# The second value head of a pair kept with its two batches exchanged

## The reference, cut to what matters

```
attn  = inverse of (I + strictly lower part of (k_beta k^T * decay))        64 x 64
w     = attn (v_beta - k_beta*g_exp state)                                  "solve"
out   = (q*g_exp) state + lower(q k^T * decay) w                            "inter" + "intra"
state = state*g_last + (k * k_decay)^T w                                    128 x 128
y     = rmsnorm(out * silu(z)) ; result += y W_out[its 128 rows]
```

## Time and profile before

| what | value |
|---|---|
| runs, us | 4985.07, 4973.11, 4982.58; median 4982.58 |
| the profiled execution, us | 4975.11; its span in the trace 4973.3 |
| mean granted TensorE clock | 0.985 of full speed |
| busy: TensorE matmuls, weight loads, DVE, ACT, GpSimd | 93%, 64%, 72%, 62%, 22% |
| instructions: matmul records, weight loads | 54288, 54320 |

### The profile page before, as it was taken

How to read it: one execution, slowest core, us unless ns; L and a number is a source line. 1 busy time by engine, 2 the same in 40 slices (tenths; PEclk the granted TensorE clock), 3 DMA queues, 4 the chain that set the end, 5 groups by cost and what they waited for, 6 DMA issues and landing times.

```text
span 4973.3 us, 144942 instructions
## 1 busy us (share of the span) xinstructions
PE 4647.1 (93%) x54288; PEld 3181.4 (64%) x54320; DVE 3576.1 (72%) x6424; ACT 3061.3 (62%) x7979; POOL 1089.0 (22%) x1064
## 2 busy tenths in 40 slices
PE   4998899999999899999999899999999899999998
PEld 2555666666666566666666566666666666666666
DVE  7554677777777577777777677777777677777775
ACT  2333666666666566666666566666666566666665
POOL 0000122222222122222222122222222222222222
PEclk8999999999999999999999999999999999999999
DMA  2111222222223222222223222222223322222221
GB/s 61 37 38 62 65 68 55 60 66 61 66 58 75 65 68 51 62 67 61 66 52 80 69 55 60 66 61 67 55 60 82 69 58 59 64 66 61 68 55 37
DMA packets 760109, 305.29 MB, mean 61 GB/s; under 512 B 672880, under 2 KB 716016, under 8 KB 749168
## 3 DMA queue, kind: packets, MB, share of 16 engines
q1 hardware_dynamic: 620144, 287.40, 23.4%
q10 hardware_dynamic: 139264, 8.42, 1.8%
HBM read 216.96 MB, written 66.07 MB: 57 GB/s over the span
## 4 chain that ended last, share of the span: by engine, by line
PE 74%; issue 9%; DVE 8%; DMA 3%; SPq 3%; ACT 2%; POOL 1%; DVEq 0%; ACTq 0%; POOLq 0%
PE pj L661 18%; PE dsb L820 8%; PE pj L656 7%; PE dsb L792 5%; PE pot L778 5%; PE pod L804 5%; PE ms L694 4%; PE pot L749 4%; PE pod L761 3%; PE ms L674 3%; PE pj L651 2%; PE ms L688 2%; PE pot L606 2%; DVE cy L1293 2%; PE dsb L811 2%
## 5 line engine op out<-in xcount | busy, mean ns | idle before, releaser
L1293 DVE SCALAR_TENSOR_TENSOR cy<-xpad,cw,cy 128x1024 f32<-128x1024 f32 x768 | 1104.9, 1445 | 7.4 <-ACT cy L1004 0.4
L661 PE MATMUL pj<-xnT,wt 128*128 128x512 f32 x2048 | 1020.3, 621 | 33.6 <-DMA cw<-in_L_attn_conv_weight 20.0
L1563 POOL TENSOR_TENSOR rout<-rin,expo 128x2 f32<-128x2 f32 x512 | 358.3, 700 | 2205.0 <-DVE rin L1438 2176.1
L1557 POOL TENSOR_TENSOR sdec<-st,gel 128x512 f32<-128x512 f32 x384 | 402.3, 1048 | 1156.5 <-DVE st L1427 953.9
L820 PE MATMUL dsb<-wo,yT 128*128 128x256 f32 x2048 | 574.8, 403 | 13.5 <-issue 12.4
L661 PEld LDWEIGHTS pj<-xnT,wt 128*128 128x128 f32 x2048 | 352.1, 191 | 362.9 <-issue 348.1
L1003 ACT ACTIVATE xpad<-pj 128x512 f32<-128x512 f32 x512 | 305.0, 596 | 358.9 <-PE pj L661 358.5
L656 PE MATMUL pj<-wt,xnT 128*128 128x256 f32 x2048 | 509.9, 392 | 0.0
L1063 ACT ACTIVATE yT<-dsb 128x256 f32<-128x256 f32 x512 | 202.2, 395 | 483.3 <-PE dsb L811 480.5
L1427 DVE TENSOR_TENSOR st<-dsb,sdec 128x512 f32<-128x512 f32 x384 | 265.3, 691 | 324.0 <-PE dsb L792 324.0
L820 PEld LDWEIGHTS dsb<-wo,yT 128*128 128x128 f32 x2048 | 348.2, 190 | 118.5 <-issue 90.4
(11 more groups left out here) (175 smaller groups left out, 8336.8 us busy)
## 6 DMA issues: line engine op xcount, KB each, us to landing
qge<-ge_rows SPq DMA_DIRECT2D x64, 1024.0 KB, 7.4
wt<-in_L_attn_W_qkvz SPq DMA_DIRECT2D x64, 768.0 KB, 4.9
gb<-g_rows SPq DMA_DIRECT2D x128, 256.0 KB
a_d<-at SPq DMA_DIRECT2D x64, 512.0 KB, 2.6
wo<-in_L_attn_W_out SPq DMA_DIRECT2D x64, 256.0 KB, 2.7
x_d<-xpair SPq DMA_DIRECT2D x128, 128.0 KB, 1.7
ap_<-a_d SPq DMA_DIRECT2D x512, 16.0 KB, 1.8
dd<-x_d SPq DMA_DIRECT2D x512, 16.0 KB, 1.9
```

What stands on the lines that cost most here:

```text
L661: last = mm(pj[n % 2][:, :], wt[:, k, col:col + DH], batch(xnT, k, i), start=(k == 0), stop=(k == KD - 1))
L1293: stt(y, x[:, :, tap:tap + SEQ], cw[:, kind, tap:tap + 1], y, ALU.mult, ALU.add).then_inc(S["conv"], 1)
L1557: tt(sdec[:, :, :, :], st[:, c % 2, :, :, :], bc(gel[:, p, :, :].rearrange("p h (b c) -> p b h c", b=NB)[:, :, :, c], 3, DH), ALU.mult).th ...
L1563: tt(rout[:, :], rin[:, :], expo[:, 0, 0:GRP], ALU.pow).then_inc(S["routs"], 1)
```

## The change

Head h = 1 of each pair keeps its values with the batches exchanged: a new function `home(b, h)` gives `b` for h = 0 and `1 - b` for h = 1. v of head 1 is convolved with its batches exchanged, z of head 1 is projected so, and w, the output and the gate live so. The decay and inverse matrices stay where they were, so that head 1's solve reads weights on rows of half a and writes to the other half: solve and intra use the corners (0,0), (0,64), (64,64), (64,0). For that the two heads' w and outputs stand in different PSUM banks; units are counted h*NC + c instead of c*GRP + h. The projection of z and the output projection of head 1 are split into half-width products that exchange the halves.

```diff
-        dsb = ctx.enter_context(nc.psum_tensor("dsb", [P, NB, 512], F32))
-        pch, pds = dsb[:, 0, :], dsb[:, 1, :]
-        pot = bank("pot")
-        pod = bank("pod")
-        pkw, po = pot, pod
+        quad = ctx.enter_context(nc.psum_tensor("quad", [P, 4, 512], F32))
+        pot, pod, pch, pds = (quad[:, n, :] for n in range(4))
+        po = quad[:, 0:2, DH:2 * DH]
+        pod_rows = quad[:, 0, 2 * DH:2 * DH + D]
+        pw = quad[:, 1:3, 0:DH]
+        pks = quad[:, 2, 0:GRP * DH]
+        pyt = quad[:, 3, 0:GRP * DH]
+        pstate = quad[:, 2:4, GRP * DH:2 * GRP * DH]
...
+        def home(b, h):
+
+            return b if h == 0 else 1 - b
...
                 elif kind == "z":
                     for v in range(2):
                         c = 2 * i + v
+                        dst = pj[n % 2][:, v * GRP * DH:(v + 1) * GRP * DH]
                         for k in range(KD):
-                            last = mm(pj[n % 2][:, v * GRP * DH:(v + 1) * GRP * DH], xnT[:, k, c * P:(c + 1) * P],
-                                      wt[:, k, 4 * DH:4 * DH + GRP * DH], start=(k == 0), stop=(k == KD - 1))
+                            mm(dst[:, 0:DH], xnT[:, k, c * P:(c + 1) * P], wt[:, k, 4 * DH:5 * DH],
+                               start=(k == 0), stop=(k == KD - 1))
+                        for k in range(KD):
+                            for b in range(NB):
+                                last = mm(dst[half(b), DH:], xnT[:, k, c * P + (1 - b) * CH:c * P + (2 - b) * CH],
+                                          wt[:, k, 5 * DH:6 * DH], start=(k == 0), stop=(k == KD - 1),
+                                          tile_position=(0, b * CH))
...
                 if r == 0:
                     loaded(pe, d_ee, g, GRP * NBLK)
-                    loaded(pe, d_et, g, GRP * NBLK)
-                    after(pe, "pneg", g, 2)
+                    after(pe, "pneg", g, 3)
...
-                        if r == 1:
-                            turned = tile_product(ms[1][half(1 - b), cut], 1 - b, pback[half(b), v, :],
-                                                  yy[half(b), 8 + v, :], b)
-                        else:
-                            rhs = yy[half(1 - b), 8 + v, :] if r else eturn[half(1 - b), v, :]
-                            turned = tile_product(ms[1][half(b), cut], b, pbd[half(1 - b), 8 + v, :], rhs, 1 - b)
+                        lhsT = pback[half(b), v, :] if r == 1 else pbd[half(b), 8 + v, :]
+                        turned = tile_product(ms[1][half(1 - b), cut], 1 - b, lhsT, src[half(b), 8 + v, :], b)
...
             def key_state(g, p, c):
...
-                for b in range(NB):
-                    last = mm(pkw[half(b), 0:GRP * DH], kq[:, p, c, b, :],
-                              st[:, c % 2, b, :, :].rearrange("p h d -> p (h d)"), start=True, stop=True,
-                              tile_position=(0, b * CH))
+                for h in range(GRP):
+                    for b in range(NB):
+                        last = mm(pks[half(b), h * DH:(h + 1) * DH], kq[:, p, c, home(b, h), :],
+                                  st[:, c % 2, home(b, h), h, :], start=True, stop=True, tile_position=(0, b * CH))
...
             def solve(g, p, c):
...
-                for h in range(GRP):
-                    for b in range(NB):
-                        rhs = rr[half(b), h, :] if c else vb[p][half(b), h, :]
-                        last = mm(pkw[half(b), (GRP + h) * DH:(GRP + h + 1) * DH], bda[half(b), p, c * GRP + h, :],
-                                  rhs, start=True, stop=True, tile_position=(b * CH, b * CH))
+                for a in range(NB):
+                    for h in range(GRP):
+                        rhs = rr[half(a), h, :] if c else vb[p][half(a), h * NC, :]
+                        last = mm(pw[half(home(a, h)), h, :], bda[half(a), p, h * NC + c, :], rhs,
+                                  start=(c == 0 or h == 1), stop=True, skip_group_check=True,
+                                  tile_position=(a * CH, home(a, h) * CH))
...
             def intra(g, p, c):
-                if c == 0:
-                    before(pe, "og", g)
                 if c == NC - 1:
                     after(pe, "wev", g, NC)
+                    after(pe, "accs", g, c - 3 + 1)
...
-                for h in range(GRP):
-                    for b in range(NB):
-                        last = mm(po[half(b), h * DH:(h + 1) * DH], it[half(b), p, c * GRP + h, :], ww[half(b), h, :],
-                                  start=(c == 0), stop=True, skip_group_check=True, tile_position=(b * CH, b * CH))
+                for b in range(NB):
+                    for h in range(GRP):
+                        last = mm(po[half(home(b, h)), h, :], it[half(b), p, h * NC + c, :], ww[half(b), h, :],
+                                  start=(c == 0), stop=True, skip_group_check=True,
+                                  tile_position=(b * CH, home(b, h) * CH))
...
-                for h in range(GRP):
-                    last = mm(dsb[:, 0, GRP * DH:GRP * DH + D], yT[:, h, :], wo[:, p, h, :],
-                              start=(h == 0), stop=(h == GRP - 1))
+                mm(pod_rows, yT[:, 0, :], wo[:, p, 0, :], start=not bank_cleared, stop=False, skip_group_check=True)
+                for b in range(NB):
+                    last = mm(pod_rows[half(b)], yT[:, 1, half(1 - b)], wo[:, p, 1, :], start=False, stop=True,
+                              skip_group_check=True, tile_position=(0, b * CH))
                 last.then_inc(S["od"], 1)
...
+                else:
+                    before(pe, "og", g)
...
-                    for v in range(2):
-                        c = 2 * i + v
-                        last = fn(vb[p][:, c * GRP:(c + 1) * GRP, :].rearrange("p h d -> p (h d)"),
-                                  src[:, v * GRP * DH:(v + 1) * GRP * DH], ACT.Copy, scale=kn[:, c:c + 1])
+                    for v in range(4):
+                        c, h = 2 * i + v // GRP, v % GRP
+                        last = fn(vb[p][:, h * NC + c, :], src[:, v * P:(v + 1) * P], ACT.Copy, scale=kn[:, h, c:c + 1])
...
+                for b in range(NB):
+                    ts(kn2[half(1 - b), 1, :], ms[1][half(b), 0:NC], L2_EPS, None, ALU.add)
...
+                if (r, n) == (0, 1):
+                    loaded(dve, d_et, g, GRP * NBLK)
+                add = eturn[:, :, :] if n and r != 1 else ee[:, us, :]
```

More of the change, by code:

```diff
@@ L760, in query_state @@
                     for b in range(NB):
-                        last = mm(po[half(b), h * DH:(h + 1) * DH],
-                                  qge[:, p, h, c * P + b * CH:c * P + (b + 1) * CH],
-                                  st[:, c % 2, b, h, :], start=(h == 0), stop=False, skip_group_check=True,
-                                  tile_position=(0, b * CH))
+                        row = c * P + home(b, h) * CH
+                        last = mm(po[half(b), h, :], qge[:, p, h, row:row + CH], st[:, c % 2, home(b, h), h, :],
+                                  start=True, stop=False, skip_group_check=True, tile_position=(0, b * CH))
                 last.then_inc(S["qs"], 1)
@@ L791, in update @@
                     for b in range(NB):
-                        last = mm(dsb[:, b, h * DH:(h + 1) * DH], kkd[p][half(b), c * GRP + h, :], ww[half(b), h, :],
+                        last = mm(pstate[:, b, h * DH:(h + 1) * DH], kkd[p][half(b), h * NC + c, :], ww[half(b), h, :],
                                   start=True, stop=True, tile_position=(b * CH, 0))
@@ L810, in output_rows, with out_project @@
                 for h in range(GRP):
-                    last = tp(dsb[:, 1, (GRP + h) * DH:(GRP + h + 1) * DH], zz[p][:, j, h, :], ident)
+                    last = tp(pyt[:, h * DH:(h + 1) * DH], zz[p][:, j, h, :], ident)
                 last.then_inc(S["yt"], 1)
-            def out_project(g, p, j):
+            def out_project(g, p, j, bank_cleared):
                 if j == 0:
@@ L850, in core_step @@
                     query_state(g, p, c)
+                else:
+                    before(pe, "og", g)
                 two, three = behind(g, p, c, 2, first), behind(g, p, c, 3, first)
                 if three:
-                    out_project(*three)
+                    out_project(*three, c > 0)
                 if two:
@@ L874, in last_tile @@
                 p = hk % 2
-                out_project(g, p, NC - 3)
+                after(pe, "og", g, NC)
+                out_project(g, p, NC - 3, False)
                 for j in (NC - 2, NC - 1):
                     output_rows(g, p, j)
-                    out_project(g, p, j)
+                    out_project(g, p, j, False)
             def weave(g, hk, first=False):
@@ L934, in column_stage @@
                 for b in range(NB):
-                    fn(colstage[half(b), :, i, :].rearrange("p k (c h) -> p k c h", h=GRP),
-                       src[:, b], ACT.Copy).then_inc(colev, 1)
```

(17 more changed lines are left out.)

53 lines of the change are left out of this document (24 added, 29 removed).

## The result

The changed kernel takes 5046.1 us, the median of 4 runs (5044.77 to 5055.03). The kernel before takes 4983.82 on the same chip (4 runs). The ratio is 1.0129, 95% interval 1.0114 to 1.0144. Forecast were 5036 us, a range of 4992 to 5088, and slower by 1.1%. The profiled execution is at 5046.87 with a span of 5045.1, so its views answer directly to those of before, whose span is 4973.3: 71.8 us are to be found. The granted clock is the same (0.986 against 0.985).

What follows compares the result with a forecast made beforehand. TensorE, its matmuls covering 93% of the span, was taken to set the time. Steps summed to +1.26 us a head, +81 over 64 heads, less 27: +54, so 5036 us as a median, slower by 1.1%, range 4992 to 5088.

Steps and rivals of the forecast that it cites:

- The changes of shape: At out_project, eight times a head: changing to column tiles and back for the transposes costs 0.15 + 0.15 = 0.30 us.
- Rival one (cheap changes): At out_project and the z fills: added shape changes are cheap, so not slower; about -110 us, 4873; chance 6%.
- The z fills on TensorE: Four z projection fills a head, each half full and half column-tiled: cost 0.55 us once and 0.40 three times.
- Four corners: Solve and intra products, 16 a head: 2 rounds instead of 4, 0.218 us less each, at most 223 us.
- The last rival: At solve and intra: corners sharing rows do not run side by side at 128 columns; +180 us, 5216; chance 3%.
- the rival of more stalls: On TensorE: more records make issue stalls grow, and the v stall is twice as long; +35 us, 5071; chance 11%.
- The v stall: Before the last v transposes: TensorE waits for ACT, with four evacuation instructions instead of two; 0.45 us a head.
- The turned blocks: First inverse round: TensorE's wait for the turned blocks' DMA moves to DVE; 27 us gained, between 12.5 and 42.
- Chunks 5 and 6: c=5, with two z fills, +0.81 us a head; c=6 -0.22, its DVE wait swallowing out_project's 0.30 and the solve's saving.
- The head's end and c=0, 1: Chunks 0 and 1, to the first square sums, +0.58 us a head including the 0.45 v stall; c=7 +0.08.
- c=3: Chunk 3, -0.11 us a head: the intra product's saving is lost in TensorE's wait for ACT at the square sums.

Runs made afterwards that it cites:

- run 1: Changed kernel with out_project's head 1 as one full matmul again, ACT exchanging the halves while copying y^T in two copies: 4965.77 us, 0.9959 of the kernel before.
- run 2: Kernel before with only out_project's head 1 split into two half-width matmuls, no halves exchanged: 5090.02 us, ratio 1.0206.
- run 7: Changed kernel with ACT emptying the v tiles in two wide instructions instead of four, head 1 taking head 0's norms: 5033.25 us, ratio 1.0098.
- run 10: Changed kernel with TensorE's wait for the DMA of the turned blocks put back ahead of the first inverse round: 5052.11 us, ratio 1.0153.
- run 4: Changed kernel with the z fills of the kernel before, ACT unchanged, so head 1's gate belongs to the wrong batch: 5042.79 us, ratio 1.0124.
- run 5: Changed kernel with both out_project and z fills in full matmuls again, ACT exchanging the halves of both: 5015.2 us, ratio 1.0076.
- run 8: Changed kernel with out_project in one shape (ACT exchanging) and DVE emptying two of the four v tiles: 4949.66 us, ratio 0.9937.
- run 9: Changed kernel with one-shape out_project, DVE emptying half the v tiles, and the z fills of the kernel before: 4961.03 us, ratio 0.9968.
- run 6: Changed kernel with solve and intra product back on two corners, head 1's values mixed between batches: 5154.65 us, ratio 1.0353.

## Why the forecast held, and which of its steps did not

**The changes of shape: right.** out_project and the transposes take 1.212 + 0.367 instead of 0.967 + 0.312, 0.300 a time as forecast. I had put 0.15 of it inside out_project and 0.15 behind it; it is 0.25 and 0.05, because the gap ahead of the transposes falls before their start. Runs 1 and 2 show from both sides that this part decides the sign. Rival one (cheap changes) is out: L825 to L827 takes 0.63, not 0.43.

**The z fills on TensorE: right.** The slot with the whole price shows 2.838 against 2.508 with a solve shortened by 0.205, so 0.535 (forecast 0.55); the others 0.435 (0.40). The column-tile rounds in the timeline, L668 in 0.59, are 4 x 0.109 and a change: their weights loads stay hidden although all tiles span the same 128 rows. By the rule of the Trainium skill that I had weighed ("TensorE: Matmul & The Clock Gate", Part 3), that a load overlaps only when the row group differs, they would not; this trace again denies it. The same part of that page of the Trainium skill also lets a load into the background weight buffer go ahead of running matmuls, which I had left out.

**Four corners: right.** 0.205 a product (0.218), at corners that share rows. The last rival is out. So is the rival of more stalls: the stops called issue are 68.5 us in all as before, and the v stall is not twice as long.

**The v stall: right in size, wrong in worth.** The timeline has 0.48 a head (0.19 ahead of the last transposes and 0.29 inside them) for 0.45. Run 7 takes it away and gains 13 us, not 29: the step that failed is that a stall of TensorE is worth its length.

**The turned blocks: the same error with the other sign.** I gave 27 for a wait of 27.8 that run 10 shows; its removal is worth about 12, with an interval from about 0 to 24. The stops called issue, of which I had taken half to be this wait, stayed at 68.5 us in total.

**Chunks 5 and 6 were the step that went wrong.** I wrote that the chain to the off-diagonal products "starts at key_state" in c=6 and swallows what is saved there, and that c=5 pays its z fills in full. c=5 did come 0.86 later, but c=6 gave 1.05 back (though out_project is 0.30 longer there), where 0.22 and 0.42 for the turned blocks were forecast, and its wait got shorter, not longer. Two things stand in the traces in its place.

The first is a chain beside TensorE (DVE products, DMA), which does not start at key_state of c=6: from there to the off-diagonal products it takes 3.71 before, 3.49 in the changed kernel, 3.95 in run 4 and 4.45 in run 5. From the square sums of c=3 it takes 21.4 to 21.6 before and in runs 1, 4, 5, 8 and 9, although c=4 and c=5 take TensorE 15.07 in run 5 and 16.04 in run 1 (22.0 from the square sums in the changed kernel). So it starts earlier; where, no run looked. Of the 0.97 that run 4 saves in c=5 alone, 0.4 is left when these products start. In runs 5 and 9 DVE's residuals hold the solves besides, for 94.5 and 94.3 us.

The second stood in my sum at nothing, and among my rivals only as a growing total: stops of TensorE at instructions that wait for nothing. Within c=6 they are 0.45 us a head before, 0.18 in the changed kernel and 0.70 in run 4 (waits for DVE 0.56, 0.35 and 0.59; for DMA 0.20, 0.06 and 0.23). Of the 1.19 by which c=6 is longer in run 4 than in the changed kernel, 0.52 is this, more than DVE and DMA together. So the z fills cost nothing at the end of this kernel, 5043 with the old fills and 5046 with the new. That the chain over DVE and DMA hides them is shown for about a third: 31 of the 86 us that come back as stops are waits for DVE and DMA. The price of 0.81 in c=5 was right as TensorE's time and wrong as the kernel's.

**The head's end and c=0, 1** came out 0.44 dearer than forecast. 0.23 of it is the intra product's saving in c=1, which goes into the wait for ACT at the square sums (36.7 us for 10.6), as I had counted for c=3 alone; the stretch of the v transposes is longer by another 0.3 than its stall, as much as the 18.0 us of stops called issue there; 0.1 was saved elsewhere. Outside the 62 heads stand 15 us where my sum puts under 3. 5 of them lie before the first solve, which comes anywhere between 532 and 541 us in the twelve kept traces; for the other 10 no run looked, and their cause stays open.

So the 1.1% was near the 1.3% in part by luck: errors of either sign (c=6 against c=0 and 1 and the parts outside, the v stall against the turned blocks) cancel. What is shown is the price list of TensorE and the roles of out_project and the corners: 80 to 105 us against 108. The prices of the parts do not add up to the result. out_project (80 to 105), z (3), the v tiles (13), the turned blocks (12 gained) and the corners (108 gained), each changed by itself, add up to something between 24 us gained and 1 lost, where the edit loses 62. So a price found for one part alone is not its share of the 62; what each part costs together with the others was not measured.

## What to carry to other kernels

A better packing of the array can be undone by the changes of tile shape that its layout brings elsewhere: count the changes, at 0.15 to 0.20 us each in this kernel, and ask whether an engine that copies the data anyway can do the exchange, as ACT did for y^T (TensorE's waits for ACT are 71.9 us there, 74.3 in the changed kernel). Where TensorE is busy 93% of the time but a chain over DVE and DMA runs nearly as long, a price read from TensorE's timeline is only an upper bound: what is taken away beside that chain can come back as stops in full (runs 4 and 9). A wait removed counts for the time only when one knows what stops the engine next, and the next stop can be the supply of the engine's own code.

## What was not expected of the hardware

The stops that the profile calls issue are 115.2 us in all in run 4, 82.7 in run 7, 68.5 in the changed kernel, 47.4 with another wait put in (run 10) and 42.7 with two corners (run 6). The number of instructions does not order them, since runs 6, 10 and the changed kernel issue the same count of matmuls within 32. The waits name no releaser, but the traces have one. These are the packets, MB and share of the DMA queue q8, which carries code, in the kernel before, the changed kernel and run 4:

```profile
q8 instruction: 455, 7.45, 0.6%
...
q8 instruction: 508, 8.32, 0.7%
...
q8 instruction: 476, 7.80, 0.6%
```

It is TensorE's code: the changed kernel has 32 packets of 16384 bytes more than run 4 for 8192 more matmul and load records, 64 bytes each, while DVE and ACT issue the same number in both. And the stops follow it. Behind the prelude, 774 stops called issue in the twelve kept traces stand at instructions that wait for nothing in the program; 713 of them end 1.1 to 1.6 us after a packet of this queue has landed. Of the same moments shifted by 7 to 28 us only 2 to 8 in a hundred do. In the changed kernel they are 55 of 62 (45.6 of 53.6 us), in run 4 78 of 88 (86.9 of 94.8 us). One of them in the timeline of run 4, a record short of the end of the off-diagonal products:

```profile
4207.04 1.09 PE L701 MATMUL pj<-dd,off 64*64 64x64 f32 x31
4209.73 0.21 PE L701 MATMUL pj<-dd,off 64*64 64x64 f32 x1 [1.59 <-issue]
```

The packet started at 4207.4 and landed at 4208.3, 1.4 before TensorE went on.

In the changed kernel 60 of the 62 stand between the solve of c=6 and the next head's first, where the products of the inverse are: 64 matmul records and their 64 loads, 8 KB of code by the 64 bytes each, in 0.95 us. Where TensorE waits there for something else, as in run 10, fewer of these stops follow. That fits code that arrives during the wait, so that the two do not add up; no run here changed the supply of code, so how much time it costs, and why its packets come late more often in one kernel than in another, stays open. The few stops that stand at an instruction with a wait (13.6 us in the changed kernel) mostly do not follow a packet, and for them nothing in the profile says what releases them.
